# A two-chunk loop on TensorE in place of 24 chunks written out, with the waits that another wait already covers left out

## The chip, the core and the metric

The kernel runs on one core of a Trainium2 chip, and the metric is the device time of one execution in microseconds. Five engines work side by side, each with its own stream of instructions: TensorE (PE in the rows; PEld is its weight load), VectorE (DVE), ScalarE (ACT), GpSimd (POOL), and SyncE (SP), which issues most of the transfers here. They order themselves by semaphores only. The program is written by hand: every instruction, wait and buffer stands in the source in the order in which it is issued.

## The reference

The input `x` is 32 x 64 x 56 x 56 in float32. Cut to what matters:

```python
x = x + conv(_ln_c(x))      # sign of the centred input, 3x3 conv with sign weights, batch norm, clip to [-1, 1]
t = to_tokens(x)            # one token per pixel, 64 features
t = t + ffn(_ln_t(t))       # mixture of 8 experts:
    feat = mean(x, axis=0)                      # over the 32 images
    w = softmax(feat @ Wr + br)                 # one gate per pixel and expert
    h = relu(bn(x @ W1[e] + b1[e]))             # layer 1, 64 -> 64, for each expert e
    h = relu(bn(h @ W2[e] + b2[e]))             # layer 2, 64 -> 64
    y = h @ Wo[e] + bo[e]                       # layer 3, 64 -> 64
    return sum over e of y * w[e]
```

## The kernel before

There are two stages. In the first, 16 pairs of images are centred, signed and convolved. TensorE runs this as a loop already, `pe.Fori(0, TWOS // 2 - 1)` at L552, of seven passes with two pairs of images each; every pass has eight times four `centre_images` matmuls (float32) and 36 `conv_images` matmuls (bfloat16). The last two pairs are written out.

The second stage is 28 chunks (`RP`), each one row of the upper and one of the lower half of the image, for all 32 images. A chunk has eight units (`UNITS`): four groups of eight images, and two quads of experts for each. For a unit TensorE issues six blocks of four 64x64 matmuls with 448 columns: `layer1` twice (L599, for the following unit), `layer2` twice (L625), `layer3` twice (L642, for the unit before). ScalarE takes layer 1 out of PSUM (`h`, L836), VectorE takes layer 2 out (`v`, L1030), and ScalarE and GpSimd add up layer 3. Each float32 matmul of the source is two weight loads and two matmuls in the trace, so a block of four shows as eight.

Between these blocks, at places fixed by the numbers of `STEADY`, stands the preparation of the next chunks (`prep`): two centring blocks (L662), the variance (L672), the router's logits (L684), the turn of the gates (L693) and the constant part (L708).

TensorE's order is this order in the source. A block begins with waits, then an increment of a semaphore such as `l1_free` that nobody waits for and that carries the waits as an instruction of its own (`EVENT_SEMAPHORE` on PEldq, the sequencer of TensorE), and then its matmuls. The waits of interest are these, where `h_done` is counted up by ScalarE and `v_done` by VectorE:

```python
# layer1(k, s, u, i)
pe.wait_ge(u_done[g // 2], k + 2)
pe.wait_ge(h_done[0], unit + 1)      # i == 1;  h_done[1], unit  for i == 0
# layer2(k, u, ab, ...), for ab == 0
pe.wait_ge(h_done[0], unit + 1); pe.wait_ge(h_done[1], unit + 1)
pe.wait_ge(v_done[0], unit + 1)
# layer3(k, u, d), for d == 0
pe.wait_ge(v_done[0], unit + 2); pe.wait_ge(v_done[1], unit + 2)
```

`body_of_chunks` calls `chunk(k, k % 2, k == 0, min(RP - 1 - k, 2))` for each k on all five engines; the second argument picks one of two buffers, so that two chunks in a row are the smallest piece that repeats. On TensorE all 28 chunks are written out, with each semaphore's value as a number in the instruction.

Of the kernel before, what the change touches and what calls it, by code (L numbers as in the profile page):

```python
# [18 lines left out]
RP = H // 2  # L19
# [14 lines left out]
UNITS = G * QUADS  # L34
# [15 lines left out]
def metaformer_kernel(nc, x, cw, gamma, beta, Wr, br, W1, b1, g1, be1, m1, v1, W2, b2, g2, be2, m2, v2, Wo, bo, out):  # L50
    with ExitStack() as ctx:
# [3 lines left out]
        def sem(name):  # L55
            return ctx.enter_context(nc.semaphore(name))
# [128 lines left out]
        wT_done = sem("wT_done")  # L185
# [12 lines left out]
        v_done = [sem(f"v_done{i}") for i in range(2)]  # L198
        centre_free = sem("centre_free")
        logits_free = sem("logits_free")  # L200
        turn_free = sem("turn_free")
        wb_free = sem("wb_free")
        l1_free = sem("l1_free")
# [14 lines left out]
        def xa_slot(m):  # L218
# [11 lines left out]
            t=(9, 15, 21, 27), x1=(16, 21, 36, 39), centre=(31, 43), power=(33, 48),  # L230
            var=52, root=54, square=56, inv=(58, 60), logits=85, gate=86, turn=89, wb=94)
        LOGITS_BETWEEN = -1
        AHEAD = Schedule(
            t=(0, 0, 0, 0), x1=(0, 0, 0, 0), centre=(), power=(),
            var=3, root=3, square=3, inv=(3, 3), logits=5, gate=6, turn=7, wb=8)
# [4 lines left out]
        def body_of_chunks(chunk):  # L240

            for k in range(RP):
                chunk(k, k % 2, k == 0, min(RP - 1 - k, 2))
# [8 lines left out]
        with nc.Block() as block:  # L252
# [255 lines left out]
            def _(pe):  # L508
# [94 lines left out]
                def layer2(k, u, ab, first, left):  # L603

                    unit, Q = UNITS * k + u, u % QUADS
                    if ab == 0:
                        for i in range(2):
                            pe.wait_ge(h_done[i], unit + 1)
                    pe.wait_ge(v_done[ab], unit + 1)
                    if ab == 0 and u == 0 and k:  # L610
                        pe.wait_ge(g_done, k + 1)
                    if ab == 0 and u == 1 and left:
                        pe.wait_ge(var_read, k + 2)
                    if ab == 1 and u == UNITS - 2 and left:
                        pe.wait_ge(logits_read, k + 2)
                    if ab == 0 and u == UNITS - 1 and left:
                        pe.wait_ge(wT_done, k + 2)
                    if ab == 1 and k == 0 and u == 0:
                        pe.wait_ge(xc_kept, 2 * STEPS)
                    if ab == 1 and left > 1 and u in (5, 7):  # L620
                        pe.wait_ge(xc_kept, STEPS * k + 2 * STEPS + (1 if u == 5 else 2))
                    pe.sem_inc(l2_free, 1)
                    for low, i in ((0, 0), (1, 1), (0, 1), (1, 0)):
                        rows_ = slice(64 * low, 64 * low + 64)
                        last = mm(ps[64 * i:64 * i + 64, L2_BANKS[ab] + low, 0:NG], w2[rows_, Q + QUADS * i, :],  # L625
                                  h[rows_, u % 2, i, ab, :], start=True, stop=True)
                    last.then_inc(z2_full[ab], 1)

                def layer3(k, u, d):

                    unit, g, Q = UNITS * k + u, u // QUADS, u % QUADS
                    if d == 0:
                        for ab in range(2):
                            pe.wait_ge(v_done[ab], unit + 2)
                        if k == 0 and u == 0:
                            pe.wait_ge(g_done, 1)
                        if Q == 0:
                            pe.wait_ge(sums_kept, G * k + g + 1)
                        pe.sem_inc(l3_free, 1)
                    for low, par in ((0, 0), (1, 1), (0, 1), (1, 0)):  # L640
                        rows_ = slice(64 * low, 64 * low + 64)
                        last = mm(ps[64 * par:64 * par + 64, ACC_BANKS + low, 0:NG], wo[rows_, 2 * Q + d, :],  # L642
                                  v[rows_, u % 2, par ^ (g % 2), d, :], start=(Q == 0 and d == 0), stop=(Q == QUADS - 1 and d == 1))
                    if d:
                        last.then_inc(l3_done, 1)

                def prep(at, q, s, h):
                    Y, Z = L2_BANKS
                    for p in places_at(at.centre, h):
                        pe.wait_ge(x1_done, G * q + 2 * p + 2 + G)  # L650
                        if q == 1 and p == 0:
                            for n in range(STEPS):
                                pe.wait_ge(u_done[n], 2)
                        elif q == 1:
                            pe.wait_ge(xc_kept, STEPS + 1)
                        else:
                            pe.wait_ge(v_done[1], UNITS * (q - 2) + (5, 7)[p] + 1)
                        pe.sem_inc(centre_free, 1)
                        for low, high in ((0, 0), (1, 1), (0, 1), (1, 0)):
                            rows_ = slice(64 * low, 64 * low + 64)  # L660
                            g = 2 * p + (low ^ high)
                            last = mm(ps[64 * high:64 * high + 64, Z + low, 0:NG], centre64[rows_, :],  # L662
                                      xin[rows_, s, BG * g:BG * g + BG, :], start=True, stop=True)
                        last.then_inc(centre_done, 1)
                    if h == at.var:
                        pe.wait_ge(xc_done, STEPS * q + STEPS)
                        if at is AHEAD:
                            pe.wait_ge(c2_done, 1)
                        if at is STEADY:
                            pe.wait_ge(v_done[0], UNITS * (q - 1) + 2)  # L670
                        for i in range(2 * STEPS):
                            last = mm(ps[32 * i:32 * i + 32, Y, 0:NG], var_ones[:], spread[:, i // 2, i % 2, :], start=True, stop=True)  # L672
                        last.then_inc(var_done, 1)
                    if h == at.logits:
                        pe.wait_ge(feat_done, q + 2)
                        bank = ACC_BANKS
                        if at is STEADY:
                            pe.wait_ge(v_done[1], UNITS * (q - 1) + UNITS - 3 + 2)
                            bank = Z
                        pe.sem_inc(logits_free, 1)  # L680
                        for par in range(2):
                            for low in range(2):
                                rows_ = slice(64 * low, 64 * low + 64)
                                last = mm(ps[0:W, bank + low, E * par:E * par + E], feat[rows_, par, :], wr[rows_, :], start=True, stop=True)  # L684
                        last.then_inc(logits_done, 1)
                    if h == at.turn:
                        pe.wait_ge(gate_done, q + 1)
                        bank = ACC_BANKS
                        if at is STEADY:
                            pe.wait_ge(v_done[0], UNITS * (q - 1) + UNITS - 2 + 2)  # L690
                            bank = Y
                        pe.sem_inc(turn_free, 1)
                        mm(ps[0:C, bank, 0:W], gate_w[:], ident[0:C, 0:W], start=True, stop=True).then_inc(wT_full, 1)  # L693
                    if h == at.wb:
                        bank = ACC_BANKS
                        if at is STEADY:
                            pe.wait_ge(v_done[0], UNITS * (q - 1) + UNITS - 1 + 2)
                            bank = Y
                        pe.sem_inc(wb_free, 1)
                        if at is AHEAD:  # L700
                            pe.wait_ge(placed_done, q + 1)
                            for hi in range(2):
                                last = mm(ps[64 * hi:64 * hi + 64, bank + 1, 0:NG], to_half[:, hi, :], placed[:].rearrange("p a w -> p (a w)"),
                                          start=True, stop=True)
                            last.then_inc(wb_full, 1)
                        pe.wait_ge(wT_done, q + 1)
                        for par in range(2):
                            last = mm(ps[64 * par:64 * par + 64, bank, 0:W], expert_const[:, 64 * par:64 * par + 64], wT[:], start=True, stop=True)  # L708
                        last.then_inc(g_full, 1)

                def chunk(k, s, first, left):
# [21 lines left out]
                        prep_point(prep, k, s, left, POINTS * u + 5)  # L733
                    if not left:
                        for d in range(2):
                            layer3(k, UNITS - 1, d)

                def first_centre(p):
                    pe.wait_ge(x1_done, 2 * p + 2 + G)
# [33 lines left out]
                prep(AHEAD, 0, 0, AHEAD.turn)  # L773
                prep(AHEAD, 0, 0, AHEAD.wb)
                prep(STEADY, 1, 1, STEADY.centre[1])
                body_of_chunks(chunk)


            @block.scalar
# [371 lines left out]
```

## Time and profile before

| | us |
|---|---|
| median of 3 runs | 1329.09 |
| lowest and highest of the three | 1326.27, 1329.15 |
| span of the profiled execution, first to last instruction | 1325.0 |
| TensorE busy in it | 1286.5 |
| ScalarE, VectorE, GpSimd busy | 878.6, 823.4, 652.2 |

The profiled execution is given by its span alone; a time of its own, as the runs have it, is not listed. The median lies 4.1 us above the span. Busy time is the time in which at least one instruction of the engine was under way. Matmuls are pipelined and their ends are modelled, so TensorE can be called busy and yet be fed too slowly: better than its busy share is the distance between starts of blocks of the same size. A row with `PEldq` is an instruction of TensorE's sequencer, such as a wait or a branch. DMA queue q8 carries instructions, not data.

### The profile page before, as it was taken

The page shows a single profiled execution, that of the slowest core. Times are in us where ns is not written, and L with a number is a line of the kernel's source. Part 1 is how long each engine was busy: PE and PEld are TensorE (multiplying, and loading weights), DVE is VectorE, ACT ScalarE, POOL GpSimd, SP SyncE. Part 2 cuts the span into 40 slices and gives each one's busy share as a digit, 9 for nine tenths or more (in the row PEclk, how much of TensorE's full clock was granted, in tenths as well). Part 3 has the DMA queues.
Part 4 walks back from the last instruction along what each step waited for, and adds up shares of the span by engine and source line. Part 5 has one row for each costly group of instructions (what it writes and reads, how often), then busy time and mean ns, then how long its engine had stood idle before and what let it go on. Part 6 is the DMA issues. An engine that isn't in the chain of part 4 may idle for free.

```text
span 1325.0 us, 37058 instructions
## 1 busy us (share of the span) xinstructions
PE 1286.5 (97%) x14956; PEld 683.8 (52%) x14956; DVE 823.4 (62%) x1470; ACT 878.6 (66%) x1120; POOL 652.2 (49%) x580
## 2 busy tenths in 40 slices
PE   6999989999999999999999999999999999999997
PEld 3777735544445544544545454544555455444454
DVE  4444666767656666566666666666666666666654
ACT  5677656666766776666766667676667676766643
POOL 0141415564565554565644555446555455555452
PEclk9999989999999999999999999999999999999999
DMA  9897403333233343243432333323333323343211
GB/s 212 203 202 195 82 15 71 78 86 81 55 78 84 80 85 76 51 87 72 86 82 51 82 74 82 86 58 71 82 81 83 72 62 84 78 83 85 54 44 29
DMA packets 262771, 112.55 MB, mean 85 GB/s; under 512 B 243336, under 2 KB 247008, under 8 KB 262624
## 3 DMA queue, kind: packets, MB, share of 16 engines
q1 hardware_dynamic: 261360, 108.87, 37.9%
q0 software_dynamic: 1264, 1.61, 0.6%
q8 instruction: 106, 1.74, 0.6%
q14 instruction: 41, 0.34, 0.1%
HBM read 84.25 MB, written 26.17 MB: 83 GB/s over the span
## 4 chain that ended last, share of the span: by engine, by line
PE 92%; issue 3%; DVE 1%; DMA 1%; POOL 1%; SPq 1%; ACT 1%; POOLq 0%; DVEq 0%
PE ps L642 26%; PE ps L599 25%; PE ps L625 24%; PE ps L544 7%; PE ps L662 3%; PE ps L529 3%; PE ps L672 2%; SPq L272 0%; DMA out<-o 0%; POOL sums L482 0%; DMA xa<-in_x 0%; PE ps L684 0%; POOL o L486 0%; DVE xin L1046 0%; POOL o L476 0%
## 5 line engine op out<-in xcount | busy, mean ns | idle before, releaser
L1030 DVE SCALAR_TENSOR_TENSOR v<-ps,negb,wb 128x448 f32<-128x448 f32 x896 | 573.1, 679 | 389.2 <-PE ps L625 387.5
L836 ACT ACTIVATE h<-ps,bias 128x896 f32<-128x896 f32 x448 | 450.0, 1005 | 274.5 <-PE ps L599 271.6
L642 PE MATMUL ps<-v,wo 64*64 64x448 f32 x3584 | 470.0, 541 | 7.3 <-issue 6.7
L625 PE MATMUL ps<-h,w 64*64 64x448 f32 x3584 | 466.7, 538 | 3.1 <-issue 2.4
L599 PE MATMUL ps<-xc,w 64*64 64x448 f32 x3584 | 465.3, 541 | 4.1 <-issue 3.7
L482 POOL TENSOR_TENSOR sums<-sums 128x448 f32<-128x448 f32 x112 | 127.5, 1138 | 331.5 <-ACT sums L842 331.5
L625 PEld LDWEIGHTS ps<-h,w 64*64 64x64 f32 x3584 | 189.3, 133 | 161.3 <-issue 129.0
L642 PEld LDWEIGHTS ps<-v,wo 64*64 64x64 f32 x3584 | 176.1, 133 | 164.0 <-issue 141.9
L599 PEld LDWEIGHTS ps<-xc,w 64*64 64x64 f32 x3584 | 161.5, 132 | 179.1 <-issue 169.1
L476 POOL TENSOR_TENSOR o<-xin,gconst 128x448 f32<-128x448 f32 x112 | 125.6, 1139 | 190.3 <-DMA out<-o 103.2
L486 POOL TENSOR_TENSOR o<-o,sums 128x448 f32<-128x448 f32 x112 | 128.0, 1142 | 8.8
L454 POOL TENSOR_TENSOR xc<-xc,spread 128x896 f32<-128x896 f32 x54 | 112.4, 2095 | 23.7 <-DMA spread<-rs_rows 23.4
L544 PE MATMUL ps<-sgn,convw 64*64 64x392 bf16 x2304 | 115.3, 328 | 3.5 <-issue 3.5
L969 DVE BATCH_NORM_STATS2 stats<-y 128x6 f32<-128x392 f16 x128 | 66.2, 560 | 76.5 <-ACT y L803 76.5
L842 ACT ACTIVATE sums<-ps 128x896 f32<-128x896 f32 x112 | 101.4, 905 | 10.5 <-PE ps L642 10.2
L544 PEld LDWEIGHTS ps<-sgn,convw 64*64 64x64 bf16 x2304 | 84.0, 106 | 34.5 <-issue 8.8
L1046 DVE SCALAR_TENSOR_TENSOR xin<-t,xin 128x448 f32<-128x448 f32 x112 | 96.0, 857 | 1.6 <-ACT t L863 1.5
L863 ACT ACTIVATE t<-y,bn 128x448 f32<-128x448 f16 x112 | 83.5, 750 | 0.0
L803 ACT ACTIVATE y<-ps 128x784 f16<-128x784 f32 x64 | 52.7, 824 | 42.3 <-PE ps L544 42.3
L852 ACT ACTIVATE xc<-ps 128x896 f32<-128x896 f32 x52 | 47.7, 917 | 24.5 <-PE ps L662 24.5
L529 PE MATMUL ps<-xa,centre 64*64 64x392 f32 x512 | 63.1, 513 | 0.6 <-DMA xa<-in_x 0.5
L463 POOL TENSOR_TENSOR feat<-xc 128x896 f32<-128x896 f32 x27 | 56.5, 2094 | 3.6
(166 smaller groups left out, 645.9 us busy)
## 6 DMA issues: line engine op xcount, KB each, us to landing
xa<-in_x SPq DMA_DIRECT2D x128, 196.0 KB, 5.1
xin<-in_x SPq DMA_DIRECT2D x224, 112.0 KB, 2.9
out<-o SPq DMA_DIRECT2D x224, 112.0 KB, 2.6
spread<-rs_rows SPq DMA_DIRECT2D x108, 224.0 KB, 4.1
wb<-gate_rows SPq DMA_DIRECT2D x54, 112.0 KB, 2.8
rs_rows<-rs SPq DMA_DIRECT2D x54, 7.0 KB
gate_rows<-wT SPq DMA_DIRECT2D x54, 1.8 KB
rows<-in_L_ffn_g POOLq DMA_DIRECT2D x2, 256.0 KB, 4.8
```

Source lines behind the costliest of these rows:

```text
L454: nc.gpsimd.tensor_tensor(xc[:, s, p], xc[:, s, p], spread[:, p], ALU.mult).then_inc(u_done[p], 1)
L476: nc.gpsimd.tensor_tensor(o[:, images, :], xin[:, s, images, :], gconst[:, s:s + 1, :].broadcast_to([P, BG, W]), ALU.add).then_inc(x1g_don ...
L482: nc.gpsimd.tensor_tensor(sums[:, 0], sums[:, 0], sums[:, 1], ALU.add).then_inc(p_sum, 1)
L486: nc.gpsimd.tensor_tensor(og, og, sums[:, 0], ALU.add).then_inc(sum_done, 1)
L529: last = mm(ps[64 * high:64 * high + 64, A_BANKS[g % 2] + low, 0:NA], centre64[rows_, :], xa[rows_, slot, low ^ high, g, :], start=True, s ...
L544: last = mm(ps[64 * high:64 * high + 64, CONV_BANKS[g % 2] + low, 0:NA], convw[rows_, tap, :], sgn[rows_, slot, top:top + KG, kx:kx + W], ...
L599: last = mm(ps[64 * two:64 * two + 64, L1_BANKS + ab, 0:NG], w1[half, P * q + C * two:P * q + C * two + C], xc[half, s, g // 2, ab ^ (g % ...
L625: last = mm(ps[64 * i:64 * i + 64, L2_BANKS[ab] + low, 0:NG], w2[rows_, Q + QUADS * i, :], h[rows_, u % 2, i, ab, :], start=True, stop=True)
L642: last = mm(ps[64 * par:64 * par + 64, ACC_BANKS + low, 0:NG], wo[rows_, 2 * Q + d, :], v[rows_, u % 2, par ^ (g % 2), d, :], start=(Q == ...
L836: A(h[:, u % 2, i], ps[:, L1_BANKS:L1_BANKS + 2, 0:NG], ACT.Relu, bias=bias[:, 0, q:q + 1]).then_inc(h_done[i], 1)
L842: A(sums[:], ps[:, ACC_BANKS:ACC_BANKS + 2, 0:NG], ACT.Copy).then_inc(sums_kept, 1)
L1030: last = V.scalar_tensor_tensor(out=v[:, u % 2, ab, d, :].rearrange("p (b w) -> p b w", w=W), in0=ps[:, L2_BANKS[ab] + d, 0:NG].rearrange( ...
```

## The change

Chunk 0 and chunks 25 to 27 stay written out. Chunks 1 to 24 (`LOOPED` is 24) become a `Fori` of twelve passes on TensorE, over two chunks each. The values that waits compare with now depend on the loop's register, so that the register is computed with (`ISA` and `REGISTER_ALU` in the order below). The loop is asked to start at slot 0 of a block of instructions (`head_slot`), and a hint for its closing branch is set at the top of each pass (`hint_back_edge`). In the blocks, `layer2` with ab = 0 no longer waits for `h_done` while another chunk follows (the two `layer1` blocks issued earlier on the same engine have waited for the same values), and `layer3` no longer waits for `v_done[0]` (`layer2` has). The wait for `wT_done` moves ahead of an increment, and the variance block gets an increment (`var_free`) of its own. No other engine's stream is changed.

```diff
+        var_free = sem("var_free")
...
+        LOOPED = (RP - 1 - 2) // 2 * 2
...
                 def layer2(k, u, ab, first, left):
 
                     unit, Q = UNITS * k + u, u % QUADS
-                    if ab == 0:
+                    if ab == 0 and (first or not left):
                         for i in range(2):
                             pe.wait_ge(h_done[i], unit + 1)
                     pe.wait_ge(v_done[ab], unit + 1)
-                    if ab == 0 and u == 0 and k:
+                    if ab == 0 and u == 0 and not first:
                         pe.wait_ge(g_done, k + 1)
...
-                def layer3(k, u, d):
+                def layer3(k, u, d, follows=True):
 
                     unit, g, Q = UNITS * k + u, u // QUADS, u % QUADS
                     if d == 0:
-                        for ab in range(2):
-                            pe.wait_ge(v_done[ab], unit + 2)
-                        if k == 0 and u == 0:
+                        if not follows:
+                            pe.wait_ge(v_done[0], unit + 2)
+                        pe.wait_ge(v_done[1], unit + 2)
+                        if isinstance(k, int) and k == 0 and u == 0:
                             pe.wait_ge(g_done, 1)
...
+                        pe.sem_inc(var_free, 1)
                         for i in range(2 * STEPS):
...
                             pe.wait_ge(v_done[0], UNITS * (q - 1) + UNITS - 1 + 2)
                             bank = Y
+                            pe.wait_ge(wT_done, q + 1)
                         pe.sem_inc(wb_free, 1)
...
-                        pe.wait_ge(wT_done, q + 1)
+                            pe.wait_ge(wT_done, q + 1)
...
-                body_of_chunks(chunk)
+                chunk(0, 0, True, 2)
+                with nc.Fori(0, LOOPED // 2, engines=[mybir.EngineType.PE], hint_back_edge=True, head_slot={mybir.EngineType.PE: 0}) as r:
+                    chunk(2 * r + 1, 1, False, 2)
+                    chunk(2 * r + 2, 0, False, 2)
+                for k in range(LOOPED + 1, RP):
+                    chunk(k, k % 2, False, min(RP - 1 - k, 2))
```

Two places of TensorE's order show it. The first is the seam between chunk 0 and chunk 1, where the loop now begins. Before (L708 the constant part, L642 layer 3, L599 layer 1, L625 layer 2; `w` is a weight, and the waits are those that the instruction carries or has just ahead of it):

```order
L708 MATMUL ps<-wT,expert_const 64x56 [waits v_done0,wT_done]
L708 MATMUL ps<-wT,expert_const 64x56
L642 MATMUL ps<-v,wo 64x448 x4
L599 MATMUL ps<-xc,w 64x448 [waits u_done0,h_done1]
L599 MATMUL ps<-xc,w 64x448 x3
L625 MATMUL ps<-h,w 64x448 [waits g_done,v_done0,h_done0,h_done1]
L625 MATMUL ps<-h,w 64x448 x3
L642 MATMUL ps<-v,wo 64x448 [waits v_done0,v_done1]
L642 MATMUL ps<-v,wo 64x448 x3
```

The same place in the changed kernel, where its L645, L601, L627 and L783 are layer 3, layer 1, layer 2 and the loop:

```order
L645 MATMUL ps<-v,wo 64x448 x4
L783 ISA
L783 UNCONDITIONAL_BRANCH
L783 BRANCH_PREFETCH_HINT
L783 ISA
L596 ISA [waits u_done0]
L601 MATMUL ps<-xc,w 64x448 [waits h_done1]
L601 MATMUL ps<-xc,w 64x448 x3
L613 REGISTER_ALU [waits v_done0]
L627 MATMUL ps<-h,w 64x448 [waits g_done]
L627 MATMUL ps<-h,w 64x448 x3
L637 ISA
```

A branch into the loop, a hint and register instructions have come in ahead of the matmuls, `h_done0` and `h_done1` are gone from layer 2, and one wait may now sit on a register instruction ahead of the matmul that carries the other.

The second place is the end of the loop's second chunk (even k), TensorE again; before, such a place reads like the first fence:

```order
L627 MATMUL ps<-h,w 64x448 [waits xc_kept]
L627 MATMUL ps<-h,w 64x448 x3
L702 REGISTER_ALU
L714 MATMUL ps<-wT,expert_const 64x56 [waits v_done0,wT_done]
L714 MATMUL ps<-wT,expert_const 64x56
L645 MATMUL ps<-v,wo 64x448 x4
L783 REGISTER_ALU
L783 COMPARE_AND_BRANCH
```

The block of layer 3 is now followed by the loop's count and its closing branch, and then either by the hint and register instructions of the head again or by chunk 25. Between head and branch there are 422 matmuls of the source (1688 weight loads and matmuls in a trace), 35 `REGISTER_ALU` and 10 `ISA`; all matmuls stand in the order in which they stood.

## Rows read from the trace of the kernel before

**Rows 1.** The page: its span, the busy time of the engines, TensorE in 40 slices.

```profile
span 1325.0 us, 37058 instructions
...
PE 1286.5 (97%) x14956; PEld 683.8 (52%) x14956; DVE 823.4 (62%) x1470; ACT 878.6 (66%) x1120; POOL 652.2 (49%) x580
...
PE   6999989999999999999999999999999999999997
...
PEclk9999989999999999999999999999999999999999
```

**Rows 2.** The page: the chain that ended last, by engine, in shares of the span.

```profile
PE 92%; issue 3%; DVE 1%; DMA 1%; POOL 1%; SPq 1%; ACT 1%; POOLq 0%; DVEq 0%
```

**Rows 3.** TensorE at an undisturbed and at a disturbed place: start, length, line, count.

```profile
388.93 1.01 PE L599 MATMUL ps<-xc,w 64*64 64x448 f32 x8
389.68 1.01 PE L625 MATMUL ps<-h,w 64*64 64x448 f32 x8
390.43 1.01 PE L642 MATMUL ps<-v,wo 64*64 64x448 f32 x8
391.18 1.01 PE L599 MATMUL ps<-xc,w 64*64 64x448 f32 x8
...
936.67 0.54 PE L642 MATMUL ps<-v,wo 64*64 64x448 f32 x1
938.77 0.60 PE L642 MATMUL ps<-v,wo 64*64 64x448 f32 x4 [1.57 <-issue]
```

**Rows 4.** Stretches: 22 chunks, then single chunks (engine busy, count; clock, DMA, GB/s).

```profile
314.00:1204.00 890.00, 879.74 (x9280) 439.71 (x9276) 575.67 (x1012) 605.61 (x770) 485.33 (x396) 1.00 0.35 76
627.58:666.68 39.10, 39.10 (x427) 20.53 (x422) 24.89 (x46) 27.40 (x35) 22.35 (x18) 1.00 0.36 76
1154.62:1194.12 39.50, 39.45 (x427) 17.09 (x423) 26.41 (x47) 27.44 (x36) 22.02 (x18) 1.00 0.37 77
1035.30:1074.80 39.50, 39.50 (x427) 19.45 (x424) 26.35 (x47) 27.74 (x36) 21.99 (x18) 1.00 0.35 78
585.29:627.58 42.29, 40.59 (x427) 18.34 (x423) 27.36 (x48) 27.59 (x36) 22.05 (x18) 1.00 0.34 75
911.42:953.94 42.52, 40.85 (x426) 22.70 (x422) 25.92 (x47) 27.36 (x36) 22.00 (x18) 1.00 0.33 72
```

**Rows 5.** DMA queues by stretch: 314 to 1204, 23 to 37, 37 to 144, 935 to 940 us.

```profile
q8 instruction: 77, 1.26, 0.6%
...
q8 instruction: 3, 0.05, 1.6%
...
q1 hardware_dynamic: 13119, 19.72, 83.8%
q0 software_dynamic: 1264, 1.61, 7.3%
q14 instruction: 3, 0.02, 0.1%
...
q1 hardware_dynamic: 1710, 0.88, 85.0%
q8 instruction: 1, 0.02, 1.4%
```

**Rows 6.** TensorE's loop L552: its register instructions and closing branch, ns min/median/max.

```profile
L552 PEldq FUSED_REGOPS  x7: 50/50/50, 14.5 to 123.8; - x7
L552 PEldq ALU_OP  x7: 32/32/32, 36.6 to 141.3; - x7
L552 PEldq COMPARE_BRANCH  x7: 76/208/238, 36.7 to 141.4; - x7
```

**Rows 7.** A pass of that loop as a stretch, columns as in rows 4.

```profile
36.70:54.10 17.40, 17.40 (x362) 12.74 (x356) 8.30 (x16) 12.41 (x18) 1.34 (x2) 1.00 0.93 206
```

**Rows 8.** Wait instructions on TensorE's sequencer, ns min/median/max, first and last start.

```profile
L595 PEldq EVENT_SEMAPHORE  x448: 51/1096/3749, 177.3 to 1308.1; - x150
...
L609 PEldq EVENT_SEMAPHORE  x143: 51/51/51, 181.0 to 1310.3; - x143
...
L638 PEldq EVENT_SEMAPHORE  x112: 51/51/51, 196.1 to 1312.9; - x112
```

More of the change, by code:

```diff
@@ L617, in layer2 @@
                         pe.wait_ge(wT_done, k + 2)
-                    if ab == 1 and k == 0 and u == 0:
+                    if ab == 1 and first and u == 0:
                         pe.wait_ge(xc_kept, 2 * STEPS)
@@ L650, in prep @@
                         pe.wait_ge(x1_done, G * q + 2 * p + 2 + G)
-                        if q == 1 and p == 0:
+                        ahead = isinstance(q, int) and q == 1
+                        if ahead and p == 0:
                             for n in range(STEPS):
                                 pe.wait_ge(u_done[n], 2)
-                        elif q == 1:
+                        elif ahead:
                             pe.wait_ge(xc_kept, STEPS + 1)
@@ L735, in chunk @@
                         for d in range(2):
-                            layer3(k, UNITS - 1, d)
+                            layer3(k, UNITS - 1, d, False)
                 def first_centre(p):
```

## The prediction

> **What bounds the kernel now.** Read the page first. TensorE is busy for 1286.5 of 1325.0 us, the next engine, ScalarE, for 878.6 us, and in all but three of the 40 slices TensorE has a 9; the granted clock is full in all but one slice [rows 1]. The chain that ended last runs over TensorE for 92% of the span, and 3% is "issue", time in which the engine waited for nothing that the profile shows [rows 2]. So the end moves only if TensorE's stream gets shorter or is fed better. The change takes no matmul away, which leaves the feeding.
>
> How well is it fed? In the timeline, blocks of eight matmuls with 448 columns start 0.75 us apart at an undisturbed place: 388.93, 389.68, 390.43, 391.18. Near 936 us one matmul of such a block starts at 936.67 and the next at 938.77, 2.10 us later, and the gap is put down to issue [rows 3]. No other engine held it there.
>
> The same in stretches of one chunk, cut from one turn of the gates (L693) to the next: the count of TensorE's matmuls is 427, give or take one, in each, but three of them last 39.10, 39.50 and 39.50 us, and two last 42.29 and 42.52 us. Over 22 chunks the mean is 890 / 22 = 40.45 us [rows 4]. The work is the same, so what differs is a loss, about 1 us per chunk on average against the good ones.
>
> What is the loss? The DMA queues name a candidate. Queue q8 carried 77 packets, 1.26 MB, in these 22 chunks, which is 3.5 packets of 16 KB in each; and one of them lies in the 5 us around the gap at 936 us, where the data queue took 85% of the 16 engines [rows 5]. These are TensorE's instructions: 9280 matmuls and 9276 weight loads in the stretch [rows 4] over 77 packets make 241 for each packet, with the waits on top. I read the gap as TensorE's sequencer at the end of what it holds, with the next packet queued behind data. Most packets do no harm, since they land while the sequencer stands at a wait: the wait ahead of layer 1 takes 1096 ns in the median [rows 8]. That is why chunks with three or four packets can still take 39.5 us.
>
> **Does a loop remove these packets?** The kernel has a loop on TensorE already. It needed three packets between 23 and 37 us, in its first pass, and between 37 and 144 us, over six more passes, q8 does not appear at all: the queues that worked there are q1, q0 and q14 [rows 5]. A pass is at most 362 + 356 = 718 weight loads and matmuls [rows 7], so 718 / 241 = 3.0 packets' worth stayed in place. Its closing branch took 208 ns in the median and 238 at most [rows 6], which is no time for a transfer. The new body has 1688 weight loads and matmuls, 1688 / 241 = 7.0 packets' worth. That three stay is shown, that seven stay is not; this is the open point of the case.
>
> The Trainium skill bears on it, in "Runtime: NRT & Kernel Launch", section "Instruction fetch mechanics": TensorE's instruction memory is given as 128 KiB, 2048 instructions, filled in blocks of 16 KiB. By that the new body would fit, with little to spare. The size of the packets agrees (16 KB); no run shows the capacity. The same section warns against this change: fetching ahead is purely sequential, only two blocks are held, and a taken branch out of them has to fetch its target. Three packets' worth without one packet in six passes speaks against "two blocks" on this engine, but not against a limit below seven.
>
> **The sum.** (1) Passes 2 to 12 of the new loop are chunks 3 to 24, about the 22 chunks from 314 to 1204 us. If no packet is fetched there, I take the mean of the three good chunks, 39.37 us: 22 x (40.45 - 39.37) = 23.8 us less. The lower bound is TensorE's idle time in the stretch, 890 - 879.74 = 10.3 us, which leaves out what the modelled ends hide. The upper bound is the best chunk throughout, 22 x (40.45 - 39.10) = 29.7 us; the best chunks had packets too, but those were hidden. (2) The first pass fetches as before: 0. (3) The branch into the loop, across padding, leaves the sequence once; I charge one gap like that at 936 us, 2.1 us, where a hidden one would cost 0. (4) Back edges, eleven taken: count 32 ns, branch 208 to 238, register setup 50 [rows 6], the hint unmeasured, bounded by the branch; at most 0.6 us each. They stand just ahead of layer 1's wait, 1096 ns in the median [rows 8], so they shorten that wait: 0. Uncovered they would be 11 x 0.6 = 6.6 us. (5) Dropped waits: one instruction of 51 ns in each of eight layer 2 and four layer 3 blocks of a chunk (L609 with its siblings, L638) [rows 8], which makes 24 x 12 x 51 ns = 14.7 us of the sequencer's time. (6) Added register instructions: 35 of 32 ns and 10 of 50 in a pass [rows 6], 1.6 us, times 12 = 19.4 us of the sequencer's time. Of (5) and (6) neither is on the path while the sequencer goes on to stand at layer 1's waits, 16 times per chunk and 1.1 us in the median; were this cover gone, the net is 4.7 us lost, and if only the savings counted, 14.7 us won. I take 0.
>
> What the dropped waits asked for had been waited for earlier on the same engine, so no block starts sooner because of that. Nothing is issued in another order, and the other engines, at most 66% busy [rows 1], only see blocks arrive more evenly.
>
> Sum: -23.8 + 2.1 = -21.7 us. On the profiled span this gives 1303.3; the median of the runs lies 4.1 us above that span, so I predict 1307. With the bounds of (1) to (6), this case reaches from -29.7 - 5 (a part of (5)) to -10.3 + 2.1 + 6.6 against 1329, that is from 1294 to 1327, and most of it lies from 1298 to 1320.
>
> **The rivals.** *The body does not stay* (the change does not do what it says). Then every pass fetches its 7 or 8 packets anew, as many as two chunks do now (7.0), and the loss of 23.8 us stays. Against it: the loop of the first stage. For it: seven is more than twice what that loop shows. If the back edge is covered by its hint, the time is 1329 + 0 to 4.7: about 1330, no measurable change. The body's places are fixed by the loop, so that gaps fall at the same blocks in every pass, which can turn out several us better or worse than the present drift.
>
> *Slower: the back edge waits for its own target.* If the body does not stay and the head has to be fetched when the branch is taken, the sequencer stands for a gap like that of 2.10 us [rows 3] or more. Of that, layer 1's wait covers 1.1 us at best. Eleven back edges cost 11 x (1.0 to 2.1) = 11 to 23 us, with nothing gained: 1340 to 1352, middle 1346. It decides as soon as the head is gone at each turn. This is what the second rule of the Trainium skill above would give; the 208 ns branch of the first loop, with its head in place, says nothing on this.
>
> *The fetches were not the loss.* If the slow chunks are slow because transfers of data are late and packets only coincide, the loop removes 77 packets and gains nothing: 1329 to 1333, with (6). Against it: at 936.67 the gap is within one block of layer 3, which has all it waits for at its first matmul, and only its feeding can split it.
>
> **How the numbers follow.** The body stays and the time falls: 0.78. It does not stay, but back edges are cheap, or fetches were not the loss: 0.10, mostly unchanged. Head fetched at each turn, or registers on the path: 0.12, slower. I call no change what lies within 0.3%, 4 us, about what a measurement of this kernel can tell: faster 0.79, same 0.08, slower 0.13. The range holds almost all of the first case and ends just before the unchanged one, 1295 to 1328; the first case alone has 1298 to 1320.
>
> **What would show it.** Right: q8 has packets up to the end of the first pass, none for the next eleven, and again for chunks 25 to 27; chunks of 39.1 to 39.6 us all through the loop, alike to 0.1 or 0.2 us, and 42 us chunks gone; no gap with issue inside a block after 314 us until the loop ends; the branch near 0.2 us. Wrong: 7 or more packets in each pass, and a gap of one place in every pass; a branch of 1 us or more; or chunks of 40.4 us without any packet, in which case my reading of the loss fails. If chunks come out below 39.1 us, the dropped waits were worth more than nothing.

## The result and the profile after

The changed kernel takes 1317.17 us in the median of four runs (1315.26 to 1318.48), against 1328.04 for the kernel before (1326.27 to 1329.15): the ratio of the runs is 0.990, with a 95% interval from 0.988 to 0.992, at whose upper end the quotient of the two medians lies. That is 10.9 us less, where 22 were forecast: inside the range, and half the size.

The page of the changed kernel, to be read against [rows 1]:

```profile
span 1314.5 us, 37305 instructions
...
PE 1273.3 (97%) x14956; PEld 639.9 (49%) x14956; DVE 828.1 (63%) x1470; ACT 878.5 (67%) x1120; POOL 652.8 (50%) x580
...
PEclk9999999999999999999999999999999999998999
...
q8 instruction: 29, 0.48, 0.2%
```

29 packets of instructions are left of 106, and TensorE's clock has a dent near the end (slice 37) that it had not, while the one of slice 6 is gone. By stretches (columns as in [rows 4]): 23 chunks, almost all of the loop; two single chunks of it; the place behind its exit; the chunk in which the loop is entered; and the one in which it has just been left.

```profile
266.20:1168.90 902.70, 902.63 (x9711) 417.25 (x9708) 607.92 (x1059) 633.08 (x806) 507.30 (x414) 1.00 0.36 77
500.10:539.30 39.20, 39.20 (x427) 18.03 (x422) 26.13 (x47) 27.51 (x35) 22.03 (x18) 1.00 0.37 78
774.50:813.70 39.20, 39.20 (x427) 18.09 (x422) 26.55 (x47) 27.51 (x35) 22.02 (x18) 1.00 0.35 76
1187.50:1194.00 6.50, 5.20 (x29) 2.41 (x32) 1.80 (x3) 1.01 (x1) 1.13 (x1) 0.50 0.68 157
221.60:266.20 44.60, 41.74 (x421) 21.33 (x419) 25.79 (x46) 27.34 (x34) 22.33 (x18) 0.96 0.31 66
1168.90:1219.00 50.10, 43.17 (x422) 21.27 (x420) 25.90 (x47) 27.85 (x36) 22.33 (x18) 0.93 0.29 61
```

Inside the loop a chunk lasts 39.20 us, time after time, and the mean of the 23 is 902.70 / 23 = 39.25 us, where it was 40.45. TensorE is idle for 0.07 us of 902.70. But the chunk around the entry takes 44.6 us and the one around the exit 50.1 us, for the same work.

The sequencer's instructions at the head and the foot of the loop (ns min/median/max, first and last start), to be read against [rows 6]:

```profile
L783 PEldq COMPARE_BRANCH  x13: 80/216/4099, 225.9 to 1173.3; - x13
L783 PEldq BRANCH_PREFETCH_HINT  x12: 31/31/45, 230.0 to 1094.9; - x12
L783 PEldq FUSED_REGOPS  x12: 50/50/50, 230.1 to 1095.0; - x12
L783 PEldq ALU_OP  x12: 32/32/32, 310.2 to 1173.3; - x12
```

The branch of 4099 ns is the first of the 13, the one into the loop at 225.9 us. The eleven back edges take 216 to 268 ns each. The queues from 314 to 1177 us have no q8:

```profile
q1 hardware_dynamic: 197422, 66.02, 35.4%
q14 instruction: 28, 0.23, 0.1%
```

And the place behind the exit in TensorE's timeline (the loop's last branch is at 1173.3 us):

```profile
1183.28 0.93 PE L627 MATMUL ps<-h,w 64*64 64x448 f32 x8
1184.03 0.93 PE L645 MATMUL ps<-v,wo 64*64 64x448 f32 x8
1188.80 1.77 PE L601 MATMUL ps<-xc,w 64*64 64x448 f32 x8 [3.84 <-issue]
1190.24 1.82 PE L627 MATMUL ps<-h,w 64*64 64x448 f32 x8
1191.74 1.82 PE L645 MATMUL ps<-v,wo 64*64 64x448 f32 x8
1193.23 1.53 PE L601 MATMUL ps<-xc,w 64*64 64x448 f32 x8
1194.54 0.97 PE L627 MATMUL ps<-h,w 64*64 64x448 f32 x8
```

TensorE stands still for 3.84 us. Then its blocks start 1.5 us apart in place of 0.75 for some 6.8 us: the granted clock is 0.50 in the stretch from 1187.5 to 1194.0, which is 1.2 of 2.4 GHz. Entry and exit each have such a gap and such a stretch (2.86 us idle and 3.4 us at half clock at the entry).

So the balance of the two profiled executions, from one turn of the gates to the next, is this: -2.7 us up to the second of these marks; +5.1 where the loop is entered (45.27 against 40.16); -27.7 over the next 23 chunks; +9.5 where it has been left (50.18 against 40.67); +0.8 in the chunk after; +4.4 from the last mark to the end (54.88 against 50.53). The sum is -10.6 us, the difference of the spans -10.5. The loop gains more than was forecast, and 19.8 us go back at places outside it. The first -2.7 us lie ahead of the loop and are no more than other executions differ by there: that mark stands at 220.9 us here, at 223.6 before, and between 221.0 and 226.4 in the profiled executions of the experiments.

### The profile page after: what moved, and what is told of

The parts are those of the page before. It is cut to its first block and busy times, and to the rows that moved or that the text cites. A ratio compares the mean times of both kernels' runs of the same rounds, so it can differ in the third digit from the quotient of the medians.

```text
span 1314.5 us, 37305 instructions
## 1 busy us (share of the span) xinstructions
PE 1273.3 (97%) x14956; PEld 639.9 (49%) x14956; DVE 828.1 (63%) x1470; ACT 878.5 (67%) x1120; POOL 652.8 (50%) x580
## 5 line engine op out<-in xcount | busy, mean ns | idle before, releaser
L601 PE MATMUL ps<-xc,w 64*64 64x448 f32 x3584 | 445.9, 542 | 12.6 <-issue 12.2
L645 PE MATMUL ps<-v,wo 64*64 64x448 f32 x3584 | 447.0, 541 | 1.8 <-issue 1.5
L627 PE MATMUL ps<-h,w 64*64 64x448 f32 x3584 | 441.0, 538 | 2.5 <-issue 2.0
L627 PEld LDWEIGHTS ps<-h,w 64*64 64x64 f32 x3584 | 168.1, 133 | 174.2 <-issue 158.7
L601 PEld LDWEIGHTS ps<-xc,w 64*64 64x64 f32 x3584 | 149.2, 132 | 196.2 <-issue 190.8
L645 PEld LDWEIGHTS ps<-v,wo 64*64 64x64 f32 x3584 | 163.2, 133 | 161.8 <-issue 143.3
L456 POOL TENSOR_TENSOR xc<-xc,spread 128x896 f32<-128x896 f32 x54 | 112.6, 2105 | 21.9 <-DMA spread<-rs_rows 21.7
L1057 DVE SCALAR_TENSOR_TENSOR xin<-t,xin 128x448 f32<-128x448 f32 x112 | 101.7, 908 | 1.6 <-ACT t L874 1.5
```

What stands on the lines that cost most here:

```text
L456: nc.gpsimd.tensor_tensor(xc[:, s, p], xc[:, s, p], spread[:, p], ALU.mult).then_inc(u_done[p], 1)
L601: last = mm(ps[64 * two:64 * two + 64, L1_BANKS + ab, 0:NG], w1[half, P * q + C * two:P * q + C * two + C], xc[half, s, g // 2, ab ^ (g % ...
L1057: V.scalar_tensor_tensor(out=xg, in0=t[:, g].rearrange("p (b w) -> p b w", w=W), scalar=2.0, in1=xg, op0=ALU.min, op1=ALU.add).then_inc(x1 ...
```

## The experiments

Theory A held that the dropped waits are worth nothing and that entry and exit have their own causes, in the placing and the hint. Its rivals stand with each run. All times are medians, each beside runs of the kernel before on the same chip (1328.7 to 1330.7), and ratios have their 95% interval.

### Without the hint

```diff
-                with nc.Fori(0, LOOPED // 2, engines=[...], hint_back_edge=True, head_slot={...}) as r:
+                with nc.Fori(0, LOOPED // 2, engines=[...], head_slot={...}) as r:
```

> The loop as in the changed kernel, but without the hint for its closing branch. Theory A (the hint turns the fetching of instructions away from what follows the loop, so that the next packet is asked for only when it is missed): the 3.84 us gap behind the loop's exit shrinks to at most 2.1 us, the half clock after it (6.8 us) goes, and the time falls by 7 to 11 us to about 1308. Theory B (the fetcher stands still during a resident loop whatever the hint says): the gap at the exit stays, 1317, give or take 1. Theory C (the hint is what keeps the head in place): eleven back edges cost 1 to 2 us each or packets come back in every pass, 1330 to 1345.

Measured: 1348.67 us, ratio 1.015 (1.013 to 1.018). Theory C, beyond its range, since a long back edge costs more than the 1 to 2 us that it had. The branches:

```profile
L783 PEldq COMPARE_BRANCH  x13: 76/223/5450, 231.3 to 1211.1; - x13
```

Back edges alternate between 0.2 us and 4.8 to 5.5 us (2nd, 4th, 6th, 8th and 10th), with 9 packets in every second pass and none in the others, 74 in all. After each long one but one the clock is at half for 3.4 us. Without the hint the head is thus gone at every second turn; with the hint it was there at all eleven. The hint is what makes this loop pay.

But theory A's sign at the exit is there too. The gap of 3.84 us and the half clock behind it are gone, and the chunk around the exit takes 43.46 us in place of 50.18. The first packet behind the last branch starts 1.3 us after it, where in the changed kernel it takes 13.0 us and the engine has run dry by then. What is left of the loss there are two gaps of 1.57 and 1.41 us at later packets, and the last stretch stays long, at 55.08. So the hint saves the turns of the loop and has a part in what the exit costs.

### Without a slot

```diff
-                with nc.Fori(0, LOOPED // 2, engines=[...], hint_back_edge=True, head_slot={...}) as r:
+                with nc.Fori(0, LOOPED // 2, engines=[...], hint_back_edge=True) as r:
```

> The loop with the hint, but not placed at slot 0 of a block, so that the code runs into its head. Theory A (the entry branch of 4.1 us and the half clock behind it are the cost of jumping across padding): the entry branch disappears or is short, the 2.86 us gap near 227 us goes and the time falls by 4 to 6 us to about 1312, if the body still stays in place. Rival (the body, 7.1 packets long, lies over nine blocks when it starts in the last part of one, and then does not stay): packets in every pass and the time back at 1325 to 1345.

Measured: 1308.80 us, ratio 0.985 (0.983 to 0.987). Theory A on the entry, with a fall of 8.4 us where 4 to 6 were expected: there are 12 branches in place of 13, none above 237 ns, and no half clock behind the entry. The body stays at this place too. The chunk of the entry takes 40.55 us in place of 45.27, so the jump across padding cost 4.7 us. The exit gets cheaper as well, which theory A did not expect: its chunk takes 44.33 us here in place of 50.18, with no half clock, and the last stretch 52.15 in place of 54.88.

### The waits alone, all written out

```diff
-                chunk(0, 0, True, 2)
-                with nc.Fori(0, LOOPED // 2, ...) as r:
...
-                for k in range(LOOPED + 1, RP):
-                    chunk(k, k % 2, False, min(RP - 1 - k, 2))
+                body_of_chunks(chunk)
```

> All 28 chunks written out as before, only the doubled waits left out and the two increments moved or added as in the change. Theory A (as predicted, the waits are worth nothing, since the sequencer stands at layer 1's wait in any case): 1328, within 2 us of the kernel before, about 105 packets in q8. Rival (less to do between blocks lets the sequencer get ahead of a late packet): 3 to 12 us less, 1316 to 1325.

Measured: 1472.13 us, ratio 1.108 (1.106 to 1.111). Neither theory: leaving out twelve waits per chunk that never made anything wait costs 143 us. The page of this run (busy time, q8, the three costliest groups of TensorE), then one gap in its timeline:

```profile
PE 1333.1 (91%) x14956; PEld 720.5 (49%) x14956; DVE 816.5 (56%) x1470; ACT 879.6 (60%) x1120; POOL 655.9 (45%) x580
...
q8 instruction: 105, 1.72, 0.5%
...
L645 PE MATMUL ps<-v,wo 64*64 64x448 f32 x3584 | 516.1, 547 | 33.2 <-issue 32.5
L627 PE MATMUL ps<-h,w 64*64 64x448 f32 x3584 | 507.2, 543 | 38.4 <-issue 37.9
L601 PE MATMUL ps<-xc,w 64*64 64x448 f32 x3584 | 507.2, 547 | 28.6 <-issue 28.3
```

```profile
513.47 0.93 PE L627 MATMUL ps<-h,w 64*64 64x448 f32 x8
514.22 0.93 PE L645 MATMUL ps<-v,wo 64*64 64x448 f32 x8
516.35 0.98 PE L601 MATMUL ps<-xc,w 64*64 64x448 f32 x8 [1.19 <-issue]
```

The number of packets is as before (105 against 106), but about 99 us of issue stand ahead of the three layers' matmuls, where the kernel before has 13. Between 240 and 1400 us the clock also falls to half nine times, for 3.4 us each. To see why, all of TensorE's instructions in the trace (weight loads, matmuls, and the sequencer's) were counted in order of start. Between 240 and 1150 us, the instruction behind each gap of over 0.9 us between two starts has a number of 13 modulo 256, in all 52 gaps of this run and in all 13 of the kernel before. A gap stands exactly where a packet of 256 instructions ends, which shows that at the gap of [rows 3] the sequencer is at the end of what it holds. What differs is how early the next packet starts to move. (The order is that of the starts in the trace, and a count is good to a few instructions: by the matmuls alone, the 13 gaps stand at 13 to 15.) This is the median count of instructions from the start of a q8 packet to the next such place, and the sequencer's own instructions in a chunk:

```
                      own instr.  all instr.  packet starts    gaps of
                      per chunk   per chunk   ahead of end by  over 0.9 us
waits left out             46        890          13              52
kernel before              58        902          55              13
```

With the waits left out, the first instruction of the new packet starts 2.2 to 2.8 us after the packet does (10th to 90th percentile). Thirteen instructions are worth 0.6 us of TensorE's time at the pace of a chunk (39.2 us for 890), 55 are worth 2.4.

The traces also settle whether such a packet is slow or late. In the kernel before, the 13 packets with a gap took 0.9 to 1.3 us on their queue, 1.10 us in the median, and the other 66 of these 910 us took 1.10 us in the median too. But the 13 had started 38 instructions ahead of the end or less, and no packet that started over 38 ahead left a gap. The one at 936 us started 2 ahead.

### The loop with the doubled waits

```diff
-                    if ab == 0 and (first or not left):
+                    if ab == 0:
...
-                        if not follows:
-                            pe.wait_ge(v_done[0], unit + 2)
-                        pe.wait_ge(v_done[1], unit + 2)
+                        for ab in range(2):
+                            pe.wait_ge(v_done[ab], unit + 2)
```

> The loop as in the changed kernel, but with the doubled waits of before. Theory A (the loop alone makes the gain, waits are worth nothing): 1317, give or take 1, chunks of 39.2 us, no packets in passes 2 to 12. Rival (the loop's register instructions need the room that the dropped waits gave): chunks get longer by 0.1 to 0.5 us, 1320 to 1330.

Measured: 1307.77 us, ratio 0.984 (0.981 to 0.986). Theory A is right on the loop (chunks of 39.2 us, no packet after the first pass) and wrong on the waits and the time: with them the whole is 9.4 us faster than the changed kernel. All of that lies behind the exit: its chunk takes 44.15 us in place of 50.18, the next 39.45 in place of 40.56, the last stretch 51.69 in place of 54.88, and there is no half clock at the exit.

From here on theory D: the next packet is asked for after a certain number of the sequencer's own instructions, whatever they do. Rival E: it is the waiting that matters.

### Increments in place of the waits

A semaphore `pace` that nobody waits for is counted up where a wait instruction fell away, in `layer2` with ab = 0 and in `layer3` with d = 0 and Q = 0, twelve per chunk:

```diff
+                    elif ab == 0:
+                        pe.sem_inc(pace, 1)
...
+                        elif Q == 0:
+                            pe.sem_inc(pace, 1)
```

> All 28 chunks written out and the doubled waits left out, which took 1472 us, but with an increment of a semaphore that nobody reads, twelve per chunk, where a wait instruction fell away: as many sequencer instructions as in the kernel before, at the same places, and they wait for nothing. Theory D (it is the number of sequencer instructions ahead of a packet's end that gives the next packet time; what they wait for does not matter): back to 1329, give or take 4. Rival E (the waits themselves hold the sequencer at the right places): 1450 to 1475.

Measured: 1327.99 us, ratio 0.999 (0.998 to 1.000). Theory D; 144 us hang on twelve instructions per chunk whose count nobody reads. Packets start 54 instructions ahead, and there are 11 gaps.

### More of them in the kernel before

```diff
                     unit, g, q = UNITS * k + u, u // QUADS, u % QUADS + QUADS * i     # layer1
+                    pe.sem_inc(pace, 1)
...
                     unit, Q = UNITS * k + u, u % QUADS                                # layer2
+                    pe.sem_inc(pace, 1)
```

> The kernel before, with an increment that nobody reads ahead of each layer 1 and layer 2 block, 32 more sequencer instructions of 51 ns per chunk. Theory D: gaps at packets' ends get rarer still, 5 to 20 us faster than before, 1309 to 1324. Theory E, or the sequencer's own time: unchanged or slower, 1329 to 1345.

Measured: 1296.39 us, ratio 0.975 (0.974 to 0.977). Theory D, and beyond its range: 32 such instructions per chunk make the kernel before 32 us faster, three times the gain of the change. Its page, its stretch from 240 to 1150 us, then the same stretch of the kernel before and of the one with the waits left out:

```profile
span 1295.3 us, 37954 instructions
...
q8 instruction: 110, 1.80, 0.6%
```

```profile
240.00:1150.00 910.00, 909.46 (x9767) 436.56 (x9762) 609.92 (x1065) 637.27 (x810) 510.17 (x416) 1.00 0.36 78
```

```profile
240.00:1150.00 910.00, 899.87 (x9487) 454.52 (x9483) 588.81 (x1032) 618.43 (x785) 498.18 (x406) 1.00 0.35 77
```

```profile
240.00:1150.00 910.00, 831.22 (x8386) 432.81 (x8376) 515.94 (x915) 546.31 (x694) 441.55 (x358) 0.99 0.31 67
```

In 910 us TensorE gets through 9767, 9487 and 8386 matmuls. The first has more packets than the kernel before (110 against 106) and not one gap of over 0.9 us between 240 and 1150 us; its packets start 47 instructions ahead of the end or more. So it is not the fetching that costs, it is the late start.

Then with 16 increments (layer 2 only) and with 64 (two ahead of each block of layers 1 and 2):

> The kernel before with an increment that nobody reads ahead of the layer 2 blocks only, 16 more sequencer instructions per chunk in place of 32. Theory D, counted: the next packet is asked for when the sequencer has handled some 11 to 12 instructions of its own in the present one (traces: 46 per chunk 13 instructions ahead of the end in the median, 58 per chunk 55 ahead, 90 per chunk 109 ahead). With 74 per chunk it should start about 85 instructions ahead, nearly no gap is left, and the time is 1297 to 1303. Rival (each such instruction gives its own small share): half of the gain, 1312.

> The kernel before with two such increments ahead of each layer 1 and layer 2 block, 64 more per chunk, where 32 gave 1296.4. Theory D: the gaps are gone already, so that nothing more is won; packets start about 150 instructions ahead, and the sequencer's own time (64 times about 0.1 us per chunk) begins to show: 1296 to 1302. Rival (more is better): under 1293.

Measured: 1298.21 us, ratio 0.975 (0.972 to 0.977), and 1299.90 us, ratio 0.977 (0.975 to 0.979). Theory D in both times. The packet distance is 87 in the first, as expected; in the second it is 171, where about 150 was expected. The table complete, with the own instructions that fall into 256 (own / all x 256) and how many of them had gone by when the packet started, (256 - distance) / 256 of that:

```
                      own    all   per 256   distance   gone by   time, us
waits left out         46    890    13.2        13        12.5     1472.1
kernel before          58    902    16.5        55        12.9     1328.7
16 increments          74    918    20.6        87        13.6     1298.2
32 increments          90    934    24.7       109        14.2     1296.4
64 increments         122    966    32.3       171        10.7     1299.9
```

Up to 32 increments the density of the sequencer's own instructions varies by a factor of 1.9, and the packet starts after 12.5 to 14.2 of them. With 64 it starts after 10.7 in the median and irregularly (a tenth of the packets 129 ahead or less, a tenth over 232), so that the count does not hold there as it stands. That the number of own instructions sets the start is shown by the time and the distance together; how the sequencer does it is not.

### Four chunks in a pass

The loop with the doubled waits, with six passes of four chunks:

> The loop with the doubled waits of before, but with four chunks in a pass, six passes, some 14.5 packets. Theory F (about eight packets stay, fifteen do not): packets come in every pass, some 85 to 105 in all, and the gain of 27 us in the loop is lost, 1325 to 1340. Rival (more than eight stay): packets in the first pass only and 1308 to 1312.

Measured: 1321.67 us, ratio 0.995 (0.993 to 0.996). The body does not stay (Theory F on the packets: 111 of them, more even than its 85 to 105), but the time is below its range, and the rival's too is missed. The loop's branches (ns min/median/max), then q8 on the page:

```profile
L782 PEldq COMPARE_BRANCH  x7: 88/4040/4373, 226.3 to 1191.6; - x7
```

```profile
q8 instruction: 111, 1.82, 0.6%
```

Each of the five back edges and the entry takes 4.0 to 4.4 us in spite of the hint, and the chunk around each is about 3 us longer than the others (42.5 against 39.2; 44.6 at the one that half clock follows). The other chunks fetch 3 or 4 packets each and still take 39.2 to 39.6 us. That fits theory D, since the loop's register instructions are the sequencer's own too: here 22.0 of 256 instructions are its own, between 16 and 32 increments in the table. So this loop gives about what the increments give, and pays it back at its turns.

### No slot and the doubled waits together

> The loop with the doubled waits of before and with no slot asked for, both of which were faster than the changed kernel alone (1307.8 and 1308.8). If their gains add up: the entry branch of 4.3 us goes, 1301 to 1304. Rival (with 24 more instructions the body starts or ends such that it lies over nine blocks): packets in every pass, 1325 to 1350.

Measured: 1305.28 us, ratio 0.983 (0.982 to 0.985), just above the range. The two gains do not add up: without a slot the doubled waits are worth 3.5 us (1308.80 to 1305.28), with the slot they are worth 9.4. The entry is free (39.5 us around it), the exit is not: 42.46 and 41.38 us for the two chunks behind it.

With increments in the chunks that stay written out:

```diff
+                    if isinstance(k, int):
+                        pe.sem_inc(pace, 1)
```

> The loop with the doubled waits and no slot (1305.3), and the extra increments in the chunks that stay written out. Theory D: the chunks around the loop lose their gaps (42.5, 41.4 and 51.4 us at its end become about 40, 39.4 and 50), which makes 1298 to 1301, no better than the increments alone without any loop (1296.4). Rival (the exit has a gap of its own that no increment cures): 1303 to 1306.

Measured: 1300.77 us, ratio 0.977 (0.974 to 0.979). As theory D has it for the whole. The chunk around the exit still takes 43.78 us, with 3.4 us at half clock, so the rival is right for that one place; but for the first, all other chunks are at 38.7 to 39.5 us, and the last stretch at 49.91.

### The changed kernel with the waits back outside the loop

```diff
-                    if ab == 0 and (first or not left):
+                    if ab == 0 and isinstance(k, int):
...
-                        if not follows:
+                        if not follows or isinstance(k, int):
```

> The changed kernel with the doubled waits back in chunks 0 and 25 to 27, which are written out, and left out only in the loop. If all that the dropped waits cost lies where packets are still fetched: as with the doubled waits everywhere, 1306 to 1309. If they matter inside the loop too: 1311 to 1317.

Measured: 1303.57 us, ratio 0.980 (0.976 to 0.984), below the first range by 2 us with runs from 1298.88 to 1306.06. So what the dropped waits cost lies in the four chunks that are written out; in the loop they can go. The chunks behind the exit take 41.34 and 38.71 us, the last stretch 49.93.

## Why the prediction was right, and where it was wrong

**What bounds the kernel** was right: TensorE's feeding. That a gap such as the one at 936 us [rows 3] is the sequencer at the end of a packet is shown by the count: 13 modulo 256, 13 times of 13, and 52 of 52. The rest of that reading, "with the next packet queued behind data", did not hold: once started, the packets with a gap were as quick as the others (1.10 us in the median), but they had started 38 instructions ahead of the end or less. Nor is it the wait ahead of layer 1 as such that makes most packets harmless; increments that wait for nothing do the same.

**The body stays**: right, and the open point is settled. Seven packets' worth stay in place with the hint, over fourteen do not. The Trainium skill, "Runtime: NRT & Kernel Launch", section "Instruction fetch mechanics", gives TensorE 2048 instructions in blocks of 256. The traces agree with the blocks, by the gaps at equal places modulo 256, and are in keeping with the 2048: a body of 1827 instructions stays, though without the hint it loses its head at every second turn, and one of 3695 does not. The same section's rule that only two blocks are held does not hold here: 7.1 blocks stay over eleven back edges, and the measurement decides.

**Term (1)** was mis-sized by little. 23.8 us were forecast over 22 chunks; over 23 it is 27.7, or 26.5 over 22. The loop's chunks last 39.20 us, between the best chunk and the mean of the three that were taken. The bound of 29.7 held. (The wider range left out the 4.7 us that terms (5) and (6) could lose; the result does not hang on it.)

**Term (3)** was too small. The entry's branch took 4.1 us in place of one gap of 2.1, and the half clock behind it was not in the sum; the chunk lost 5.1 us. Leaving out the slot gives 8.4 us back in all, of which 4.7 at the entry and most of the rest behind the exit.

**Term (4)**: 0, right. Back edges take 0.2 us and chunks with and without one last the same.

**Terms (5) and (6)** failed at the sentence "I take 0". The step counted what the instructions cost the sequencer and what they wait for, and did not ask what else they do. The more instructions of its own the sequencer has in a packet, the earlier the next packet starts; with twelve fewer per chunk the packets of the written-out chunks come too late. With these waits back outside the loop, the chunk of the exit falls from 50.18 to 41.34 us and the last stretch from 54.88 to 49.93. The loop with all doubled waits is at 1307.77 and its gain is 21.5 us. The two halves of the change, which the prediction took as one gain and one nothing, are a gain of 21 and, with the slot, a loss of 9 to 11.

That the sum of -21.7 meets the gain of the loop alone is in part luck: in that run's profile the 23 chunks gain 28.4 us where 23.8 were taken for 22, and its entry and exit lose 4.5 and 3.5 us where 2.1 and nothing were taken. **The exit** was given no term of its own.

**The rivals.** "Fetches were not the loss" is refuted for the late ones and right for the others: fetches that start in time cost next to nothing, as 110 of them in 1296 us show, but late ones are the loss. "The back edge waits for its own target" is what happens without the hint and with four chunks in a pass. The 1348.67 us of the first are close to the rival's middle of 1346 by luck: five long back edges of 4.8 to 5.5 us, not eleven of 1 to 2.1.

What stays open is the exit. In one run with increments there, its chunk still takes 43.78 us. Counted as above, the first packet behind the loop's last branch starts this long after the branch, and this many instructions ahead of the end of the 256:

```
                                  us behind   instructions
                                  the branch  ahead of end
changed kernel                       13.0           0
doubled waits                        10.0           1
doubled waits outside the loop       10.0          19
no slot                               5.6           3
no slot, doubled waits                4.8           0
the same, increments outside          3.2           1
no hint                               1.3         208
four chunks in a pass, with hint      1.5         130
```

Where the hint is set and the body stays, this packet starts when the engine runs dry or little ahead of it, however many own instructions have gone by (26 in the run with increments). With four chunks in a pass it starts after 15 own instructions, as theory D has it, and without the hint already after 4. So the first packet behind such a loop does not follow the count of theory D. By what means the hint does this is not shown.

## What to carry to other kernels

When the busiest engine shows gaps by issue inside a block that waits for nothing, count its instructions in order of start: if the gaps stand at one place modulo 256, the engine is short of instructions, and the question is how early the next packet starts. In this kernel's stream of matmuls with few waits it started late, and a few increments per packet's worth were worth more than any loop: 16 or 32 per chunk gave 32 us, the loop of two chunks with its hint 11 to 25 without them. A loop costs at its ends, too: look at the chunks around its entry and its exit. Before doubled waits are cleared out of such a stream, put an increment in their place and measure both.

## What the runs showed of the hardware that was not expected

- In straight code a packet of TensorE's instructions (256 of them, 16 KB) started after 12.5 to 14.2 of its sequencer's own instructions had gone by in the present 256, for 13.2 to 24.7 of these per 256 (after 10.7 for 32.3), and with the waits left out it took 2.2 to 2.8 us from the packet's start to its first instruction.
- Behind a loop that stays in place with its hint, the first packet started 0 to 3 instructions ahead of the end in five runs and 19 in one; without the hint, 208.
- Twelve instructions of 51 ns per chunk, which wait for nothing, decide over 144 us (1472.1 against 1328.0).
- A taken branch whose target was not in place took 3.9 to 5.5 us; one whose target was, 0.2 us.
- The gaps of 2.86 and 3.84 us in the changed kernel were followed by 3.4 and 6.8 us at half clock (1.2 GHz), which adds about half of that time again, 1.7 and 3.4 us; the gap of 2.10 us near 936 us in [rows 3] was not. The length of the gap alone does not decide: with four chunks in a pass, of six gaps of 2.9 to 3.3 us only the last was followed by half clock, and without a slot one of 2.38 us was not and one of 2.46 us was.
